# Edge sort of a four-layer graph network: where the spare copies, the norm rows and the factors run, and which bits lie next to each other

## The chip, the cores and the metric

One Trainium2 chip, one core. The metric is the device time of one execution of the whole kernel in microseconds. The kernel runs four graph layers in one launch.

## The reference

100000 nodes have 64 features each; 50000 edges come with a source, a target (sorted by target) and 16 attributes. Four layers follow each other, every one with a residual and a normalization over the 64 features:

```python
edge_index = jnp.stack([src, dst])
x = _layernorm(x + _L0_gnn_ref(x, L0_gnn_W, L0_gnn_c, edge_index), axis=-1)
x = _layernorm(x + _L1_gnn_ref(x, src, dst, L1_gnn_W1_1, L1_gnn_W2_1, L1_gnn_W1_2, L1_gnn_W2_2), axis=-1)
x = _layernorm(x + _L2_gnn_ref(x, edge_index, L2_gnn_W, L2_gnn_att_src, L2_gnn_att_dst, L2_gnn_bias), axis=-1)
x = _layernorm(x + _L3_gnn_ref(x, edge_index, edge_attr_16, batch0, L3_gnn_W, L3_gnn_a), axis=-1)
```

The first layer is an attention in hyperbolic space (it needs, for every node, a chain of norms, tanh and artanh), the second a convolution, the third and fourth attentions with a softmax over the edges that share a target. All of them need sums over the edges of one source or of one target. That is why the kernel sorts the edges once at its start: the stages behind it walk edges in sorted order.

## The kernel before, in words

The change lies in one stage, `order_edges`, from 73 to some 1385 us of the trace. Ahead of it the inputs' constants are set up; behind it come the edge stages of the four layers, whose code is the same in both kernels. The next stage begins with POOL's gathers from the table `T` by edge (lines 1892 and 1895).

**Two sorts.** The edges are sorted by source (order 1, first) and by target (order 0). 65536 slots lie as 128 partitions x 512 columns; each slot has a key and two payload words (the other end, and a contribution of the attributes), in `sort_key` and `sort_load`. A bitonic network of 16 levels has 136 steps; both sorts make 272 steps. `class Network` (line 344) lists the steps as (level, bit) and gives the distance of partners within a row; `COLUMN_BIT` (line 341) says which column bit stands for which bit of the slot number. A bit that is a partition bit is brought into the columns by a **turn**: TensorE transposes 12 blocks of 128 x 128 (line 923 for the key) and ScalarE lands them back in SBUF (`land`, lines 986 to 994). There are 28 turns.

**One step on VectorE** (`order_keys` line 640, `order_loads` line 656): `swap` = low > high (line 652), the two new halves of the key by min and max (653, 654), then two predicated copies of the payload: low <- high where swapped (665), high <- `sort_spare` where swapped (667). `sort_spare` is a copy of the low half made beforehand, by ScalarE (`spare_copy`, line 1001; in a turn's step the landing writes it too, line 992). At the start of each level `flip` (lines 631, 634, 638) computes a sign and multiplies the key by it.

**Work beside the sort.** The first layer needs statistics of every node: 98 chunks of 1024 nodes pass through TensorE (`turned_rows`, `projected`, `added`, `nodes`) and ScalarE (`x_rows` line 1007, squares, `sums_out`, `nodes_out`). A table of steps sets the order by hand: chunk m begins at step `pass_step(m)` = 2m + m//8, and each engine walks the 272 steps and puts the pieces of the chunks behind the step's own work. Every 7 chunks form a batch (`batch_scales` line 737, `batch_roots`), then their **norm rows** (the normalized x of 1024 nodes) are made: 2 chunks of 3 by ScalarE (line 1043, eight activations each), one by VectorE (line 744, `by_vector`). When all batches are done, VectorE computes the **factors** of all nodes (line 754): a chain of 102 VectorE instructions over 128 x 784, some of which hand a function to ScalarE and wait for it. That is step 215 (`FACTORED`).

**Filing.** SP issues the transfers by the same table of steps: chunk loads (`pr_x`), x rows into the table `T` and one id column per chunk (`file_x`, lines 540 and 541, 4-byte words from `sort_node_f`), norm rows in and out (`pl_x`, `X`), factor columns. After a sort `rank` (line 669) puts keys and payload in plain order, `file_keys` (line 487) stores them by three DMAs and reads neighbours back, and `lay_out` (line 677) makes indices from them. For the first sort that is step 145 (`LAID`). It yields `home_row`; POOL then writes 393 times 128 words into `T` (`file_homes`, line 164), which needs all x rows and id columns filed. The stage ends when VectorE has laid out the second sort, POOL's home writes have landed and SP's transfers are done.

## Time and profile before

| | |
|---|---|
| three runs, us | 8039.57, 8034.38, 8027.68 |
| median of the runs, us | 8034.38 |
| the profiled execution: span, us | 8027.0 |
| busy over the span: VectorE / POOL / TensorE / ScalarE | 69% / 66% / 37% / 36% |
| mean DMA rate | 108 GB/s |

All rows below come from the profiled execution of the one core. Engines: PE is TensorE, PEld its weight load, DVE VectorE, ACT ScalarE, POOL GpSimd, SP the queue that issues most transfers. L665 is line 665 of the kernel. A row of the timeline has the start in us from the span's begin, the duration, engine, line, operation, output <- inputs, shape, and in brackets the idle time ahead of it with what ended it. The sort stage is the first sixth of the span, so shares over the whole span say little of it; the rows are taken from its own stretches.

### The profile page before, as it was taken

Reading aid. Unit: us, or ns where it says so; the run is one execution under the profiler, and the core shown is the slowest. Engines: PE = TensorE matmul, PEld = TensorE weight load, DVE = VectorE, ACT = ScalarE, POOL = GpSimd, SP = SyncE. Lnnn points to the kernel's source line nnn. Section 1 sums busy time; section 2 is a strip of 40 time slices with the busy share of each in tenths; the row PEclk is TensorE's granted clock in tenths of the full one; section 3 lists DMA queues with packets and bytes.
Section 4 is the critical chain, followed back from the end, with each engine's and each line's share of the span. In section 5 each row is a group of like instructions: output and inputs, shape, how many; then the busy total and the mean of one; then the engine's idle time right before and its main releaser. Section 6 shows DMA issues by size and latency. Waiting matters only on the chain. (4 is left out here: it accounts for less than half of the span.)

```text
span 8027.0 us, 77025 instructions
## 1 busy us (share of the span) xinstructions
PE 2987.5 (37%) x14049; PEld 2387.9 (30%) x14049; DVE 5509.6 (69%) x16229; ACT 2914.7 (36%) x6536; POOL 5303.4 (66%) x5145
## 2 busy tenths in 40 slices
PE   4776700211111115766656635454400000263322
PEld 1222200211111115666646634454400000252221
DVE  6667687877767756777779969999734444473764
ACT  3555523433333334444435536666500000121211
POOL 0003773777777767777757737777567777777677
PEclk9888855555555557778856655555555555576555
DMA  9884218111111114555569944444321111663321
GB/s 101 110 117 98 68 18 63 27 26 26 26 25 25 25 39 141 168 163 167 160 212 327 328 159 148 146 151 151 126 62 44 45 45 45 132 226 114 97 91 61
DMA packets 786581, 864.04 MB, mean 108 GB/s; under 512 B 469875, under 2 KB 483427, under 8 KB 779804
## 3 DMA queue, kind: packets, MB, share of 16 engines
q1 hardware_dynamic: 572556, 684.47, 30.9%
q0 software_dynamic: 163408, 175.42, 10.5%
q10 hardware_dynamic: 50240, 0.60, 0.6%
q14 instruction: 321, 2.63, 0.1%
q8 instruction: 56, 0.92, 0.1%
HBM read 419.15 MB, written 480.23 MB: 112 GB/s over the span
## 5 line engine op out<-in xcount | busy, mean ns | idle before, releaser
L164 POOL DMA_INDIRECT T<-slot_at,home_row x393 | 434.4, 1105 | 818.4 <-DVE home_row L728 677.9
L1244 POOL DMA_INDIRECT e_other<-X,index x392 | 428.1, 1092 | 177.3 <-issue 117.4
L1232 POOL DMA_INDIRECT e_ahead<-XA,index x392 | 416.3, 1062 | 178.6 <-issue 118.8
L1892 POOL DMA_INDIRECT e_mine<-T,index x392 | 392.3, 1001 | 206.1 <-issue 114.3
L3012 POOL DMA_INDIRECT e_got<-G,index x392 | 411.6, 1050 | 176.7 <-issue 112.9
L3634 POOL DMA_INDIRECT out_rows<-e4s_out,index x392 | 416.8, 1063 | 165.2 <-issue 118.8
L2383 PE MATMUL e_turned<-ident,e_own_x 128*128 128x128 f32 x196 | 54.6, 434 | 1229.4 <-DVE e_own_x L1971 1229.4
L1904 POOL DMA_INDIRECT X<-e_row,index x392 | 419.0, 1069 | 125.3 <-issue 118.8
L2532 POOL DMA_INDIRECT e_got<-X,index x392 | 413.6, 1055 | 119.5 <-issue 119.5
L2529 POOL DMA_INDIRECT e_mine<-X,index x392 | 404.4, 1032 | 130.4 <-issue 119.2
L3443 POOL DMA_INDIRECT rows<-X,index x392 | 395.6, 1009 | 130.6 <-issue 130.6
L1255 POOL DMA_INDIRECT XA<-e4d_sent,index x392 | 391.0, 998 | 119.4 <-issue 118.8
L1244 POOL DMA_INDIRECT e4d_other<-X,index x392 | 376.1, 959 | 136.1 <-issue 118.2
L1895 POOL DMA_INDIRECT e_other<-T,index x392 | 385.2, 983 | 119.5 <-issue 119.5
L2383 PEld LDWEIGHTS e_turned<-ident,e_own_x 128*128 128x128 f32 x196 | 35.1, 217 | 1240.0 <-DVE e_own_x L1971 970.6
L665 DVE COPY_PREDICATED sort_load<-sort_swap,sort_load 128x512 f32<-128x512 int32 x272 | 229.8, 845 | 250.3 <-ACT sort_spare L1001 213.7
L1703 ACT ACTIVATE e_z<-e_mine,e_share 128x64 f32<-128x64 f32 x1572 | 380.7, 334 | 35.2 <-DVE e_share L1563 35.0
L1776 PE MATMUL e_back<-w_heads,e_z_t 128*128 128x66 f32 x1600 | 329.8, 401 | 121.2 <-ACT e_z_t L1712 121.2
L1783 PE MATMUL e4d_spread<-e4d_diag,ones 128*128 128x128 f32 x2 | 0.8, 502 | 976.7 <-DVE e4d_diag L1603 976.7
L1776 PEld LDWEIGHTS e_back<-w_heads,e_z_t 128*128 128x128 f32 x1600 | 321.1, 311 | 137.9 <-ACT e_z_t L1712 106.2
L1765 PE MATMUL e_z_turned<-ident,e_z 128*128 128x128 f32 x800 | 181.1, 420 | 457.0 <-DVE e_z L1586 457.0
L1521 DVE SCALAR_TENSOR_TENSOR e_state<-e_state,e_ex,e_pay 128x64 f32<-128x64 f32 x1568 | 320.9, 279 | 0.0
(685 smaller groups left out, 13023.6 us busy)
## 6 DMA issues: line engine op xcount, KB each, us to landing
XA<-e_n_xa SPq DMA_DIRECT2D x49, 1056.0 KB, 5.5
SUMS<-e_state SPq DMA_DIRECT2D x49, 1056.0 KB
e4n_n_xa<-XA SPq DMA_DIRECT2D x49, 1056.0 KB, 5.3
X<-e_n_row SPq DMA_DIRECT2D x49, 576.0 KB
X<-pl_x SPq DMA_DIRECT2D x98, 268.0 KB, 3.0
e_n_x<-X SPq DMA_DIRECT2D x49, 536.0 KB
B<-e_n_b SPq DMA_DIRECT2D x49, 528.0 KB
e_n_b<-B SPq DMA_DIRECT2D x49, 528.0 KB
```

The lines of the kernel that those rows point to most:

```text
L164: gp.indirect_dma_start(out=words, out_offset=bass.IndirectOffsetOnAxis(ap=home_row[:, t:t + 1], axis=0), in_=slot_at[:, t:t + 1], in_offs ...
L1232: gp.indirect_dma_start(out=ahead[:, b, j, :], out_offset=None, in_=g.XA[0:SLOTS, :], in_offset=bass.IndirectOffsetOnAxis(ap=index_of(g, 0 ...
L1244: gp.indirect_dma_start(out=other[:, h, j, :], out_offset=None, in_=others[:, :], in_offset=bass.IndirectOffsetOnAxis(ap=index_of(g, s, 1, ...
L1255: gp.indirect_dma_start(out=target[:, :], out_offset=bass.IndirectOffsetOnAxis(ap=index_of(g, s, 2, n, j), axis=0), in_=sent[:, h, j, :], ...
L1776: last = t.matmul(back[:, j // 4, (j % 4) * (D + 2):(j % 4 + 1) * (D + 2)], lhsT=z_t[:, 2 * j + q, :], rhs=g.w_heads[:, q, :], start=(q == ...
L1892: gp.indirect_dma_start(out=mine[:, h, j, :], out_offset=None, in_=g.T0[:, :], in_offset=bass.IndirectOffsetOnAxis(ap=index_of(g, s, 0, n, ...
L1904: gp.indirect_dma_start(out=g.X1[:, :], out_offset=bass.IndirectOffsetOnAxis(ap=index_of(g, s, 2, n, j), axis=0), in_=row[:, h, j, :], in_ ...
L2529: gp.indirect_dma_start(out=mine[:, h, j, :], out_offset=None, in_=g.X1[:, :], in_offset=bass.IndirectOffsetOnAxis(ap=index_of(g, s, 0, n, ...
L2532: gp.indirect_dma_start(out=got[:, h, j, :], out_offset=None, in_=g.X1[:, :], in_offset=bass.IndirectOffsetOnAxis(ap=index_of(g, s, 1, n, ...
L3012: gp.indirect_dma_start(out=got[:, h, j, :], out_offset=None, in_=g.G2[:, :], in_offset=bass.IndirectOffsetOnAxis(ap=index_of(g, s, 1, n, ...
L3443: gp.indirect_dma_start(out=g.rows[:, n * J + j, :], out_offset=None, in_=g.X3[:, :], in_offset=bass.IndirectOffsetOnAxis(ap=index_of(g, s ...
L3634: gp.indirect_dma_start(out=out_rows[:, :], out_offset=bass.IndirectOffsetOnAxis(ap=index_of(g, s, 2, n, j), axis=0), in_=out[:, h, j, :], ...
```

## The change

Parts, all within `order_edges` and `Network`:

1. **Spare copies on VectorE.** The copy of the low half is now a VectorE instruction behind `swap` (new line 690); in a turn's step it follows the key's max, once the last word has landed. ScalarE's `land` has three activations instead of five.
2. **Which bits lie close.** A level's steps now use the partition order up to level 9 and the turned order above it only for the bits that then need it; the two shortest distances, 1 and 2, occur in 12 of the 272 steps (60 before). The turns stay 28. Blocks of a turn are now taken (`block`) or landed (`laid`) with a stride of four columns, in one of the two directions.
3. **Norm rows** are all on ScalarE; VectorE's two instructions per chunk (lines 744 on) are gone, and the order of ScalarE's side work around turns is changed.
4. **Passes are spread**: `pass_step(m)` = 2m + 2m//5 instead of 2m + m//8.
5. **Factors in two halves**, at steps 124 and 241, of 128 x 392 each, instead of one at step 215. Factor columns follow each half.
6. **Filing.** `file_keys` is issued from ScalarE's queue, with four part DMAs for each of the three tables. SP issues one id column per step (`blank_homes`) and the x rows on every other step; POOL's home writes wait for the id columns alone.

```diff
+    @staticmethod
+    def by_column(level, m):
+        return level > IN_COLS and m >= BY_COLUMN
...
     def distance(self, n):
-        m = self.steps[n][1]
-        return 1 << (m - IN_COLS if m >= IN_COLS else COLUMN_BIT[m])
+        level, m = self.steps[n]
+        if not self.by_column(level, m):
+            return BLOCKS << m if m < BY_COLUMN else 1 << (m - BY_COLUMN)
+        if m < IN_COLS:
+            return P << (m - BY_COLUMN)
+        return BLOCKS << (m - IN_COLS) if m < LEVELS - 2 else 1 << (m - LEVELS + 2)
...
     def pass_step(m):
-        return 2 * m + m // 8
+        return 2 * m + 2 * m // 5
...
-    FACTORED = batch_step(CH // BATCH - 1) + 2
+    HALF = CH // 2
+    FACTORED = [batch_step(HALF // BATCH - 1) + 2, batch_step(CH // BATCH - 1) + 2]
...
-                engine.dma_start(table.rearrange("(p t) a -> p (t a)", p=EC), ordered[0:EC, w, :]).then_inc(written[s], 16)
-            engine.wait_ge(written[s], 16 * 5)
+                for h in range(FILED):
+                    rows = table[h * LANES * COLS:min((h + 1) * LANES * COLS, EP), :].rearrange("(p t) a -> p (t a)", t=COLS)
+                    engine.dma_start(rows, ordered[h:h + BLOCKS * (rows.shape[0] - 1) + 1:BLOCKS, w, :]).then_inc(written[s], 16)
+            engine.wait_ge(written[s], 16 * (2 + 3 * FILED))
...
                 for n in range(-8, STEPS):
                     for m in passed(n + 8):
                         x_in(m)
-                        for c in range(3 * m // 2, min(3 * (m + 1) // 2, CH)):
-                            file_x(c)
+                    if 0 <= n < CH:
+                        blank_homes(n)
+                    if 0 <= n < 2 * CH and n % 2:
+                        file_x(n // 2)
...
-                gp.wait_ge(filed_x, 16 * (2 * CH + 1))
+                gp.wait_ge(home_blank, 16 * CH)
                 gp.wait_ge(home_rows, 1)
...
                     compared.done(v.tensor_tensor(net.kept(swap[:, :].unsqueeze(1), n)[:, 0], low[:, 0], high[:, 0], ALU.is_gt), "swap")
+                    if n not in turns:
+                        spare_copy(n)
                     compared.done(v.tensor_tensor(new_low[:, 0], low[:, 0], high[:, 0], ALU.min), "low_key")
                     compared.done(v.tensor_tensor(new_high[:, 0], low[:, 0], high[:, 0], ALU.max), "key")
+                    if n in turns:
+                        v.wait_ge(landed.sem, landed.after(turns[n], "contrib"))
+                        spare_copy(n)
+
+                def spare_copy(n):
+                    copied.done(v.tensor_copy(net.kept(spare[:, :, :], n), net.halves(load[net.order(n)][:, :, :], n)[0]))
...
-                        copy = a.activation(net.kept(spare[:, w:w + 1, :], n), net.halves(turned[:, 1 + w:2 + w, :], n)[0], ACT.Copy)
-                        landed.done(a.activation(load[s][:, w, :], turned[:, 1 + w, :], ACT.Copy), name)
-                    copied.done(copy)
+                        landed.done(a.activation(net.laid(load[s][:, w, :], n), net.landing(turned[:, 1 + w, :]), ACT.Copy), name)
...
+                    if n in turns:
+                        land(n)
+                        side_work(n - 1)
+                    if n + 1 not in turns:
+                        side_work(n)
+                    if n == LENGTH + 2:
+                        file_keys(a, 1)
+                file_keys(a, 0)
```

How instructions move, at three places. The first is VectorE in steps 46 and 47 (level 10, bits 8 and 7), before: two steps of five instructions each. `sort_swap` is the mask, `sort_spare` the copy of the low half, `sort_load` the payload.

```order
L652 TENSOR_TENSOR sort_swap<-sort_key 128x256
L653 TENSOR_TENSOR sort_key<-sort_key 128x128x2
L654 TENSOR_TENSOR sort_key<-sort_key 128x128x2
L665 COPY_PREDICATED sort_load<-sort_swap,sort_load 128x256x2
L667 COPY_PREDICATED sort_load<-sort_swap,sort_spare 128x256x2
L652 TENSOR_TENSOR sort_swap<-sort_key 128x256
L653 TENSOR_TENSOR sort_key<-sort_key 128x256
L654 TENSOR_TENSOR sort_key<-sort_key 128x256
L665 COPY_PREDICATED sort_load<-sort_swap,sort_load 128x512
L667 COPY_PREDICATED sort_load<-sort_swap,sort_spare 128x512
```

The same steps on VectorE now:

```order
L680 TENSOR_TENSOR sort_swap<-sort_key 128x256
L690 COPY sort_spare<-sort_load 128x512
L683 TENSOR_TENSOR sort_key<-sort_key 128x256
L684 TENSOR_TENSOR sort_key<-sort_key 128x256
L699 COPY_PREDICATED sort_load<-sort_swap,sort_load 128x2x256
L701 COPY_PREDICATED sort_load<-sort_swap,sort_spare 128x2x256
L680 TENSOR_TENSOR sort_swap<-sort_key 128x256
L690 COPY sort_spare<-sort_load 128x512
L683 TENSOR_TENSOR sort_key<-sort_key 128x2x128
L684 TENSOR_TENSOR sort_key<-sort_key 128x2x128
L699 COPY_PREDICATED sort_load<-sort_swap,sort_load 128x4x128
L701 COPY_PREDICATED sort_load<-sort_swap,sort_spare 128x4x128
```

The copy has come into VectorE's own queue, and the runs of neighbouring elements (2 in the first step before) are 256 and 128 long.

The second place is ScalarE around the first turn, before. `sort_turned` are the transposed blocks, `pr_xt` a chunk's rows on their way to TensorE, `pl_x` norm rows.

```order
L1007 ACTIVATE pr_xt<-pr_turned,eps 128x512
L989 ACTIVATE sort_key<-sort_turned 128x512
L992 ACTIVATE sort_spare<-sort_turned 128x256
L993 ACTIVATE sort_load<-sort_turned 128x512
L992 ACTIVATE sort_spare<-sort_turned 128x256
L993 ACTIVATE sort_load<-sort_turned 128x512
L1043 ACTIVATE pl_x<-pl_x,pl_offset,pl_inverse 128x64 x8
```

And now:

```order
L1024 ACTIVATE pr_xt<-pr_turned,eps 128x512
L1060 ACTIVATE pl_x<-pl_x,pl_offset,pl_inverse 128x64 x8
L1015 ACTIVATE sort_key<-sort_turned 128x512
L1018 ACTIVATE sort_load<-sort_turned 128x512 x2
L1046 ACTIVATE node_stats<-pr_by_node 128x40
L1042 ACTIVATE pr_sums<-pr_summed 10x512
```

A turn's landing is three activations, and the side work of the step before the turn follows it.

The third place is SP in the middle of the first sort, before. `pr_x` is a chunk's load, `T<-in_x` x rows, `T<-sort_node_f` an id column, `pl_x` and `X` the norm rows in and out.

```order
L501 DMA pl_x<-in_x 128x512
L501 DMA pr_x<-in_x 128x512
L540 DMA T<-in_x 1024x64
L541 DMA T<-sort_node_f 1024x1x1
L501 DMA pl_x<-in_x 128x512
L516 DMA X<-pl_x 128x536
L501 DMA pr_x<-in_x 128x512
L540 DMA T<-in_x 1024x64
L541 DMA T<-sort_node_f 1024x1x1
L540 DMA T<-in_x 1024x64
L541 DMA T<-sort_node_f 1024x1x1
```

And now:

```order
L522 DMA pl_x<-in_x 128x512
L560 DMA T<-sort_node_f 1024x1x1 x2
L564 DMA T<-in_x 1024x64
L522 DMA pl_x<-in_x 128x512
L537 DMA X<-pl_x 128x536
L522 DMA pr_x<-in_x 128x512
L560 DMA T<-sort_node_f 1024x1x1 x2
L564 DMA T<-in_x 1024x64
L537 DMA X<-pl_x 128x536
L522 DMA pr_x<-in_x 128x512
```

Id columns now come two for one row copy.

## Rows read from the trace of the kernel before

**Rows 1.** Windows of two stretches of the sort: busy time by engine, clock, DMA.
```profile
core 0: us, PE busy (x) PEld busy (x) DVE busy (x) ACT busy (x) POOL busy (x), PEclk, DMA share, GB/s
73.00:723.00 650.00, 463.31 (x1384) 172.89 (x1385) 459.63 (x874) 352.78 (x831) 0.09 (x1) 0.86 0.87 111
...
1019.00:1166.00 147.00, 1.86 (x8) 1.46 (x8) 131.16 (x110) 19.55 (x22) 114.18 (x99) 0.50 0.02 2
```
**Rows 2.** Groups of VectorE, 73 to 1364 us: busy, mean ns, idle ahead.
```profile
L665 DVE COPY_PREDICATED sort_load<-sort_swap,sort_load 128x512 f32<-128x512 int32 x272 | 229.8, 845 | 250.3 <-ACT sort_spare L1001 213.7 <-ACT sort_load L993 35.5
...
L771 DVE TENSOR_SCALAR sort_work<-sort_work 128x784 f32<-128x784 f32 x25 | 14.5, 581 | 4.4 <-ACT sort_work L1051 3.7
...
L634 DVE TENSOR_SCALAR sort_sign<-sort_bit 128x512 f32<-128x512 int32 x31 | 13.4, 433 | 1.1
```
**Rows 3.** Timeline at 98 us: start, us, engine, line, idle before.
```profile
98.68 0.61 ACT L1001 ACTIVATE sort_spare<-sort_load 128x512 f32<-128x512 f32 x1
...
99.39 0.71 DVE L665 COPY_PREDICATED sort_load<-sort_swap,sort_load 128x512 f32<-128x512 int32 x1 [2.45 <-ACT sort_spare L1001]
```
**Rows 4.** Timeline of VectorE in an undisturbed step, 1356 us.
```profile
1356.50 0.43 DVE L652 TENSOR_TENSOR sort_swap<-sort_key 128x256 int32<-128x256 f32 x1
1356.84 0.42 DVE L653 TENSOR_TENSOR sort_key<-sort_key 128x256 f32<-128x256 f32 x1
...
1359.05 0.43 DVE L652 TENSOR_TENSOR sort_swap<-sort_key 128x256 int32<-128x256 f32 x1
```
**Rows 5.** Line 164, POOL's home writes: shortest/median/longest ns, first and last start.
```profile
L164 POOL DMA_INDIRECT T<-slot_at,home_row x393: 966/1021/1947, 722.9 to 1296.8; - x197
```
**Rows 6.** Tile sort_load, its second predicated copy and its ranking copy.
```profile
L667 DVE COPY_PREDICATED sort_load<-sort_swap,sort_spare x272: 696/727/1311, 76.4 to 1363.4; 128x512 f32<-128x512 int32 x136
...
L674 DVE COPY sort_work<-sort_load x4: 598/603/606, 678.4 to 1365.2; 128x512 f32<-128x512 f32 x4
```
**Rows 7.** Timeline of POOL where the next stage begins.
```profile
1384.80 0.99 POOL L1892 DMA_INDIRECT e_mine<-T,index  x1 [87.00 <-DVE e_state L1928]
1386.09 0.95 POOL L1895 DMA_INDIRECT e_other<-T,index  x1 [0.30 <-issue]
```
**Rows 8.** Timeline of VectorE at a level's start, 1306 us: flip, then the predicated copy.
```profile
1306.41 0.42 DVE L631 TENSOR_SCALAR sort_bit<-sort_gray 128x512 int32<-128x512 int32 x1
...
1307.93 0.73 DVE L665 COPY_PREDICATED sort_load<-sort_swap,sort_load 128x512 f32<-128x512 int32 x1
```
**Rows 9.** Timeline at a turn, 1336 us.
```profile
1336.57 1.97 PE L923 MATMUL sort_turned<-ident,sort_load 128*128 128x128 f32 x8 [1.43 <-DVE sort_load L667]
...
1339.54 1.30 DVE L665 COPY_PREDICATED sort_load<-sort_swap,sort_load 128x512 f32<-128x512 int32 x1 [1.82 <-ACT sort_load L993]
```
**Rows 10.** Timeline of VectorE: the factors' first instruction, and the next step's swap.
```profile
1023.97 1.54 DVE L776 TENSOR_TENSOR sort_work<-node_stats 128x784 f32<-128x784 f32 x1
...
1165.99 0.43 DVE L652 TENSOR_TENSOR sort_swap<-sort_key 128x256 int32<-128x256 f32 x1 [0.22 <-DVE node_cols L771]
```
**Rows 11.** Timeline of VectorE where the first sort is laid out.
```profile
716.32 0.28 DVE L688 TENSOR_SCALAR lay_diag<-ident,sort_work 128x128 f32<-128x128 f32 x1
```
**Rows 12.** DMA issues, 73 to 723 us: engine, op, count, KB each, us to landing.
```profile
T<-in_x SPq DMA_DIRECT2D x92, 256.0 KB, 8.5
pr_x<-in_x SPq DMA_DIRECT2D x69, 256.0 KB
X<-pl_x SPq DMA_DIRECT2D x50, 268.0 KB, 3.7
pl_x<-in_x SPq DMA_DIRECT2D x52, 256.0 KB, 6.5
T<-sort_node_f SPq DMA_DIRECT2D x93, 4.0 KB, 8.9
```
**Rows 13.** Groups of ScalarE, 73 to 1364 us: the norm rows.
```profile
L1043 ACT ACTIVATE pl_x<-pl_x,pl_offset,pl_inverse 128x64 f32<-128x64 f32 x528 | 181.3, 426 | 5.0 <-DMA pl_x<-in_x 5.0
```
**Rows 14.** Groups of POOL beside the factors, 1019 to 1166 us.
```profile
L164 POOL DMA_INDIRECT T<-slot_at,home_row x99 | 114.2, 1153 | 32.8 <-issue 32.8
```
**Rows 15.** Line 1007, ScalarE's row copies of the 98 passes: first and last start.
```profile
L1007 ACT ACTIVATE pr_xt<-pr_turned,eps x98: 662/662/693, 72.8 to 995.2; 128x512 f32<-128x512 f32 x98
```

More of the change, by code:

```diff
@@ L338, in set_up @@
     sem.clear()
-COLUMN_BIT = (7, 8, 2, 3, 4, 5, 6, 0, 1)
+BY_COLUMN = 7
+BLOCKS = COLS // P
+LANES = P // BLOCKS
+FILED = -(-EC // LANES)
 class Network:
@@ L375, in kept, with block, laid, landing @@
         return tile.rearrange("p w (g d) -> p w g d", d=self.distance(n))
+    def block(self, tile, n, b):
+        if self.by_column(*self.steps[n]):
+            return tile.rearrange("p (c b) -> p b c", b=BLOCKS)[:, b, :]
+        return tile[:, b * P:(b + 1) * P]
+    def laid(self, tile, n):
+        if self.by_column(*self.steps[n]):
+            return tile.rearrange("p (b c) -> p b c", b=BLOCKS)
+        return tile.rearrange("p (c b) -> p b c", b=BLOCKS)
+    def landing(self, blocks):
+        return blocks.rearrange("p (b c) -> p b c", b=BLOCKS)
 def order_edges(nc, g, src, dst, l3_a, attr, x, sem):
@@ L398, in normed @@
         return [m for m in range(CH) if 23 + 5 * m // 2 == n]
-    FACTORED = batch_step(CH // BATCH - 1) + 2
-    assert FACTORED + CH // 2 < STEPS and all(23 + 5 * m // 2 >= batch_step(m // BATCH) + 2 for m in range(CH))
+    HALF = CH // 2
+    FACTORED = [batch_step(HALF // BATCH - 1) + 2, batch_step(CH // BATCH - 1) + 2]
+    assert FACTORED[1] + HALF // 2 < STEPS and all(23 + 5 * m // 2 >= batch_step(m // BATCH) + 2 for m in range(CH))
     def passed(n):
@@ L658, in order_loads @@
                     v.wait_ge(compared.sem, compared.after(n, "swap"))
-                    if n in turns:
-                        v.wait_ge(landed.sem, landed.after(turns[n], "contrib"))
                     v.wait_ge(copied.sem, copied.after(n))
@@ L884, in _ @@
                 for n in range(STEPS):
-                    if n == FACTORED:
-                        v.wait_ge(scaled.sem, scaled.after(CH // BATCH - 1, "offset"))
-                        factors()
+                    if n in FACTORED:
+                        half = FACTORED.index(n)
+                        v.wait_ge(scaled.sem, scaled.after((half + 1) * HALF // BATCH - 1, "offset"))
+                        halves_asked.append(len(asked))
+                        factors(half)
                     order_keys(n)
@@ L915, in turn @@
                     for b in range(COLS // P):
-                        last = t.transpose(turned[:, 0, b * P:(b + 1) * P], key[s][:, (n - 1) % 2, b * P:(b + 1) * P], g.ident[:, :])
+                        last = t.transpose(turned[:, 0, b * P:(b + 1) * P], net.block(key[s][:, (n - 1) % 2, :], n, b), g.ident[:, :])
                     turned_pe.done(last, "key")
@@ L988, in land @@
                     a.wait_ge(turned_pe.sem, turned_pe.after(k, "key"))
-                    landed.done(a.activation(key[s][:, (n - 1) % 2, :], turned[:, 0, :], ACT.Copy), "key")
+                    landed.done(a.activation(net.laid(key[s][:, (n - 1) % 2, :], n), net.landing(turned[:, 0, :]), ACT.Copy), "key")
                     for w, name in enumerate(("other", "contrib")):
                         a.wait_ge(turned_pe.sem, turned_pe.after(k, name))
-                        copy = a.activation(net.kept(spare[:, w:w + 1, :], n), net.halves(turned[:, 1 + w:2 + w, :], n)[0], ACT.Copy)
-                        landed.done(a.activation(load[s][:, w, :], turned[:, 1 + w, :], ACT.Copy), name)
-                    copied.done(copy)
-                def spare_copy(n):
-                    if n:
-                        a.wait_ge(compared.sem, compared.after(n - 1, "high"))
-                    else:
-                        a.wait_ge(made, 5)
-                    copied.done(a.activation(net.kept(spare[:, :, :], n), net.halves(load[net.order(n)][:, :, :], n)[0], ACT.Copy))
+                        landed.done(a.activation(net.laid(load[s][:, w, :], n), net.landing(turned[:, 1 + w, :]), ACT.Copy), name)
                 def x_rows(m):
@@ L1044, in norm_rows, with side_work @@
                     x1_act.done(last)
-                a.wait_ge(x1_ones, 3)
-                for n in range(STEPS):
-                    if n == FACTORED:
-                        for i, (out, x_in, f, f_scale, f_bias) in enumerate(asked):
-                            a.wait_ge(to_act, i + 1)
-                            a.activation(out, x_in, f, bias=f_bias, scale=f_scale).then_inc(from_act, 1)
-                    if n in turns:
-                        land(n)
-                    else:
-                        spare_copy(n)
+                def side_work(n):
                     for m in passed(n - 6):
@@ L1067, in _ @@
                     for m in normed(n):
-                        if not by_vector(m):
-                            norm_rows(m)
+                        norm_rows(m)
+                a.wait_ge(x1_ones, 3)
+                for n in range(STEPS):
+                    if n in FACTORED:
+                        half = FACTORED.index(n)
+                        for i in range(halves_asked[half], (halves_asked + [len(asked)])[half + 1]):
+                            out, x_in, f, f_scale, f_bias = asked[i]
+                            a.wait_ge(to_act, i + 1)
+                            a.activation(out, x_in, f, bias=f_bias, scale=f_scale).then_inc(from_act, 1)
+                    if n in turns:
[6 more added lines that the diff above has]
+                file_keys(a, 0)
     sem.clear()
```

87 lines of the change are left out of this document (37 added, 50 removed).

## The prediction

> **What bounds the kernel now.** I read the stretches of the sort stage first [rows 1]. From 73 to 723 us VectorE works 459.6 of 650 us, ScalarE 352.8 and TensorE 463.3: no engine is full, so something waits. The groups say for what: the first predicated copy of a step (L665) has 250.3 us of VectorE's idle time ahead of it, 213.7 of them until ScalarE's spare copy [rows 2]. One such wait [rows 3]: the spare copy stands in ScalarE's queue behind a pass's row copies, starts at 98.68, and VectorE resumes at 99.39 after 2.45 us. So VectorE's 272 steps are tied to ScalarE's pass work. An undisturbed step takes 2.55 us from swap to swap [rows 4] and 2.57 over the distances from 4 up.
>
> A second chain runs beside it. POOL's 393 home writes (L164) begin when step 145 has laid out the first sort, at 722.9, and the last starts at 1296.8 [rows 5]; the sort goes on to 1363.4 [rows 6], and the next stage's first gather starts at 1384.80 [rows 7]. POOL sits idle 87 us before that. So the stage now ends with VectorE, and POOL is 87 us behind it. The question is when each chain ends after the change.
>
> **VectorE up to step 145.** From the first swap at 73:
> - 146 steps x 2.57 = 375 us.
> - Spare copies: each frees VectorE after its duration less 0.08, as the swap's 0.43 does after 0.34 [rows 4]. Before shows no VectorE spare copy. The nearest rows are a one-input pass over 512 elements, 0.433 (L634) [rows 2], and a copy of 512 that gathers with a stride, 0.603 (L674) [rows 6]. Nearly all new distances have runs of 4 or more, so I take 0.43: 146 x 0.35 = 51; at 0.60 it is 25 more. The 213.7 us of waiting goes with them.
> - Rare bits: a predicated copy is 1.31 at distances 1 and 2 against 0.73 [rows 6], 1.17 us for a step's two. Steps at these distances fall from 60 to 12. Six lie here: 7. The 48 that go save 56 us over both sorts.
> - 20 sign flips, 1.52 each (from 1306.41 to the predicated copy at 1307.93) [rows 8]: 30, as before.
> - 14 turns: the predicated copy waits 1.82 us for the landed words [rows 9], and the key's landing adds some 0.4. ScalarE now lands three tiles instead of five, but VectorE's copy follows the last: I keep 2.2 each, 31.
> - 8 batch scales at about 1: 8.
> - Half of the factors. The whole is 142.0 us (1023.97 to 1165.99) [rows 10]: 102 VectorE instructions in a chain. 0.433 us for 512 and 0.581 for 784 [rows 2] give 0.15 fixed, 0.19 with the gap. So half costs (142 - 19)/2 + 19 = 81, and 85 with ScalarE's round trips, whose fixed part is not halved. The two halves cost 28 more than the whole did; the first now lies ahead of POOL's start.
> - Ranking and layout: 8 (the layout alone from 716.32 to 722.9) [rows 5, 11].
>
> Sum 595, so 668 without a wait. What can be late now is TensorE at a turn, for want of x rows. Before, 356 transfers of the five kinds listed took 0.87 of 650 us of the DMA engines [rows 1, 12], 1.6 us each. In steps 0 to 97 the new SP order issues 98 id columns, 49 row copies, 45 pass loads and some 60 norm transfers: 252 x 1.6 = 400 us, against 98 steps at 3.4 = 333 us and a prefetch of 8 steps, 27 us. That is up to 40 us of stall; zero if the 4 KB id columns cost less than the mean. I take 20, and 10 for turns that meet TensorE amid a pass: **home rows at about 700** (668 to 740).
>
> **ScalarE.** 33 more norm rows x 8 activations x 0.343 (the 0.426 each [rows 13], overlapped) add 91 us, and the 244 spare copies and 56 half ones leave it. VectorE sheds 64 products and sums of norm rows in exchange. Both lie off the path except through the pass loop (below). Keys filed from ScalarE's queue cost 9 more issues per sort, about 3.5 us; the first sort's are covered by seven steps (some 20 us) ahead of the layout, the last by POOL. If POOL were earlier, 3.5 us would show.
>
> **POOL.** 393 writes. Beside the factors, where VectorE is 89% busy, 99 took 1.153 + 0.33 = 1.485 us each [rows 1, 14]; gathers of the next stage stand 1.29 apart [rows 7]. VectorE will be nearly full, so I take 1.485: 584, and 6 for landing: **end at 1290**. The next gather follows in about 6 us (the last landing, the barrier, a few clears): 1296.
>
> **VectorE's own end.** From 700, 126 steps x 2.92 = 368, shorts 7, 11 flips 17, 14 turns 31, batches 6, the other half 85, waits 10: 1224. The tail behind the last step is 21 us before (1363.4 + 0.7 to 1384.8) and 3.5 more now: 1248. POOL ends last.
>
> So the stage closes 1384.8 - 1296 = 89 us sooner; later stages compute the same tables and I leave them. The profiled span is 8027.0, 7.4 us under the median of 8034.4; against the median: 8034.4 - 89 = **7945 us**.
>
> **Rivals.**
> - *VectorE still ends the stage* (0.12). If writes come at 1.36 us or less, POOL is done by 1248. For: POOL's pace without VectorE beside it is 1.29. Against: with VectorE at 89% it was 1.485. Time 8034.4 - 137 = 7898.
> - *The spare copies hold POOL back* (0.12). About one copy of 0.43 falls on every two writes. If each held a write by half its length or so, a write takes 1.60: 700 + 629 + 12 = 1341, time 7990. For: the writes are longest beside the factors, which have many one-input operations (1.153 against a shortest of 0.966) [rows 5, 14]. Against: 39 of those in 142 us moved the mean by only a little. The Trainium skill (SBUF — State Buffer, Who interferes with whom) says that a VectorE copy in its two-port mode takes the port pair that POOL needs to write DMA descriptors, and that the later one blocks fully. By that rule each meeting costs the rest of the copy, about this rival's time; the trace shows the direction, not the size.
> - *The pass loop is slowed, and this is slower* (0.07). The first half of the factors needs 49 passes. With p us per pass, home rows are at 73 + 49p + 12 (last batch) + 85 + 22 steps at about 3.6 (80) + 7 = 257 + 49p, and the stage ends 596 later. That passes 1384.8 from p = 10.9. At 12 the time is 8090. Before, p was (995.2 - 72.8)/97 = 9.5 [rows 15]. For: all norm rows now stand in ScalarE's queue, and DMA may starve the loop. Against: ScalarE no longer waits for VectorE at each step.
> - *It does not do what it says* (0.04): copies at 0.60 and waits of 80 us put home rows at 775, the end at 1371 and the time within 16 us of before.
>
> **Numbers.** The forecast case has 0.65. Its own range is 7885 (home rows 675, writes at 1.41) to 8000; the lock rival and VectorE's end lie inside, so 7885 to 8008 leaves out the slower rival and the edge of the last. 0.2% is 16 us, about what a measurement of this kernel tells from no change: faster by more 0.88, within 0.05, slower 0.07.
>
> **What would show it.** Right: no idle time of L665's successor until ScalarE except at 28 turns; a COPY of about 0.43 x272 on VectorE; first home write near 700; writes near 1.49 apart, the last near 1285; VectorE done 40 us or more before the next gather, then idle until POOL. Wrong: home writes start after 760 (the pass loop or DMA), writes at 1.6 (the port), or VectorE still busy when POOL is done.

## The result, and the profile after

The changed kernel takes 7921.16 us (median of four runs, 7918.86 to 7926.57) against 8033.76 before: a ratio of 0.9864, interval [0.985, 0.9878]. The forecast was 7945 in a range of 7885 to 8008. The profiled execution has a span of 7919.9 us, 107.1 less than before. Both chains of the sort stage moved: the home rows are there at 679.3 instead of 722.9, the second sort is ranked at 1196.8 instead of 1364.2, and the next stage's first gather starts at 1267.16 instead of 1384.80 [rows 7], 117.6 sooner. The later stages, whose code is the same, gave back 10.5 of it, a little here and there.

Windows of the changed kernel: busy time by engine, TensorE's clock, DMA share, GB/s, as in [rows 1].

```profile
73.00:420.00 347.00, 256.56 (x857) 98.10 (x856) 308.37 (x657) 204.52 (x497) 0.00 (x0) 0.93 0.85 117
73.00:679.00 606.00, 381.92 (x1242) 145.02 (x1242) 529.03 (x1085) 321.81 (x775) 0.00 (x0) 0.85 0.69 103
```

VectorE now works 529 of 606 us up to the home rows, where it worked 459.6 of 650. The groups of VectorE from 73 to 1364 us show what became of the wait [rows 2]:

```profile
L699 DVE COPY_PREDICATED sort_load<-sort_swap,sort_load 128x512 f32<-128x512 int32 x272 | 201.3, 740 | 2.9
L690 DVE COPY sort_spare<-sort_load 128x512 f32<-128x512 f32 x272 | 125.9, 463 | 25.3 <-ACT sort_load L1018 25.2
```

The 250.3 us of idle time ahead of the first predicated copy are 2.9. What is left, 25.2, stands ahead of the copy in the 28 turns. The copies cost 125.9 us in all. One undisturbed step, in the timeline:

```profile
126.85 0.42 DVE L680 TENSOR_TENSOR sort_swap<-sort_key 128x256 int32<-128x256 f32 x1
127.19 0.42 DVE L690 COPY sort_spare<-sort_load 128x512 f32<-128x512 f32 x1
...
129.80 0.43 DVE L680 TENSOR_TENSOR sort_swap<-sort_key 128x256 int32<-128x256 f32 x1
```

It is 2.95 us from swap to swap, against 2.55 [rows 4]. POOL's home writes and the gather behind them, by line and in the timeline [rows 5, 7] (where a distance between writes is given below, it is the last start less the first, over 392):

```profile
L164 POOL DMA_INDIRECT T<-slot_at,home_row x393: 967/1091/1721, 679.3 to 1257.7; - x197
```

```profile
1267.16 0.99 POOL L1916 DMA_INDIRECT e_mine<-T,index  x1 [8.52 <-DVE e_state L1952]
```

Before, POOL stood idle for 87 us here; now for 8.52. VectorE had laid out the second sort at 1218 and waited 47 us. **POOL ends the stage**, as forecast.

One thing was not forecast. ScalarE's queue around the filing of the first sort's keys, and what VectorE did meanwhile:

```profile
639.20 2.57 ACTq L513 DMA_DIRECT2D contribs<-sort_work  x4
647.60 1.53 ACTq L516 DMA_DIRECT2D sort_work<-keys  x3
...
651.94 0.69 ACT L1024 ACTIVATE pr_xt<-pr_turned,eps 128x512 f32<-128x512 f32 x1 [15.05 <-issue]
...
654.65 0.50 DVE L774 RECIPROCAL pl_inverse<-pl_inverse 128x56 f32<-128x56 f32 x1 [12.88 <-ACT pl_inverse L1052]
```

Between the stores (L513) and the read-backs (L516) ScalarE waits until the stores have landed. It does no other work for 15.05 us. Behind that wait stand the roots of the batch of step 139, and VectorE needs them: it waits 12.88 us at 654.65, on the path to the home rows.

### The profile page after: what moved, and what is told of

Same layout as the page of the kernel before. It is cut to its first block and busy times, and to the rows that moved or that the text cites. A ratio compares the mean times of both kernels' runs of the same rounds, so it can differ in the third digit from the quotient of the medians.

```text
span 7919.9 us, 77310 instructions
## 1 busy us (share of the span) xinstructions
PE 2935.9 (37%) x14049; PEld 2367.6 (30%) x14049; DVE 5526.6 (70%) x16542; ACT 2879.4 (36%) x6509; POOL 5343.8 (67%) x5146
## 5 line engine op out<-in xcount | busy, mean ns | idle before, releaser
L1789 PEld LDWEIGHTS e_z_turned<-ident,e_z 128*128 128x128 f32 x800 | 162.7, 225 | 461.1 <-DVE e_z L1610 384.0
```

## The experiments

The time before varied from 8032.9 to 8039.9 us between the chips of the groups, so times are compared by their ratio to the kernel before on the same chip. "After" is the changed kernel, from which every experiment starts; they are called e1 to e12 in the order in which they stand.

### The spare copies back on ScalarE

```diff
-                    if n not in turns:
+                    if n not in turns and not (n < STEPS):
                         spare_copy(n)
...
+                def spare_copy(n):
...
+                    copied.done(a.activation(net.kept(spare[:, :, :], n), net.halves(load[net.order(n)][:, :, :], n)[0], ACT.Copy))
...
+                    elif n < STEPS:
+                        spare_copy(n)
```

> Only the place of the spare copies is put back: in the 244 steps without a turn ScalarE makes them, as before the change; everything else is as changed. Theory (VectorE was tied to ScalarE's pass work): a step falls from 2.92 to 2.57 us, but the waits come back. Before they were 213.7 us over 272 steps, 0.79 each, so 132 plain steps of the first sort lose 0.44 each, 58 us: home rows at about 735 instead of 679.3, time about 7975 (7950 to 8010). Rival (the gain came from the bits and the halved factors, and the spread passes leave ScalarE time enough): no waits, 132 x 0.35 = 46 us gained, home rows at about 633, time about 7875.

Measured: 7959.0 us, ratio 0.9902 [0.9886, 0.9919], some 30 us slower than after. The group of VectorE (73 to 1300 us) and POOL's two rows:

```profile
L699 DVE COPY_PREDICATED sort_load<-sort_swap,sort_load 128x512 f32<-128x512 int32 x272 | 202.8, 746 | 186.0 <-ACT sort_spare L1025 182.5
```

```profile
L164 POOL DMA_INDIRECT T<-slot_at,home_row x393: 969/977/1650, 723.5 to 1276.5; - x197
```

```profile
1299.26 0.99 POOL L1925 DMA_INDIRECT e_mine<-T,index  x1 [21.80 <-DVE e_state L1961]
```

The waits come back, 182.5 us of the 213.7 before, and the home rows are 44 us later (58 expected). The rival, that spread passes leave ScalarE time enough, falls. But the writes stand 1.4106 us apart instead of 1.4755, and the stage is now ended by VectorE: POOL is idle for 21.8 us. That gave a suspicion on the copies, which two further runs took up.

### The order of the bits back

`Network`, the slot numbers, `rank` and the key filing as before; `block`, `laid` and `landing` without a stride.

> Only the order of the bits is put back: 60 steps at distances 1 and 2 instead of 12, plain blocks in the turns, key filing in three DMAs. Theory (price of a short distance 1.17 us a step): 24 more such steps in the first sort, 28 us, and 24 spare copies that gather with a stride, 0.18 more each, 4: home rows at about 711, last write and stage end 32 later, time about 7953 (7945 to 7960). Rival (the strided landing and block reads of the turns cost as much as the short distances save): home rows within 8 us of 679.3, time 7915 to 7930.

Measured: 7938.4 us, ratio 0.9873 [0.9857, 0.989].

```profile
L164 POOL DMA_INDIRECT T<-slot_at,home_row x393: 969/1092/1717, 690.2 to 1271.6; - x197
```

The home rows are 10.9 us later, a third of the 32 of the theory, and more than the rival's 8. The price of a short step was right: a predicated copy takes 1.29 to 1.30 at distances 1 and 2, and the 24 more such steps cost 28 us. But other waits shrank: outside the factors VectorE's plain steps of the first sort lost 25 us (ranking and layout included) instead of 42. The plain landings are also cheaper. Two rows of ScalarE's groups, 73 to 679 us, of this kernel and of after:

```profile
L997 ACT ACTIVATE sort_load<-sort_turned 128x512 f32<-128x512 f32 x28 | 16.2, 596 | 18.8 <-PE sort_turned L928 18.8
```

```profile
L1018 ACT ACTIVATE sort_load<-sort_turned 128x512 f32<-128x512 f32 x28 | 22.2, 855 | 7.7 <-PE sort_turned L949 7.6
```

On average the landing of a tile costs 0.26 us more. Only every other turn writes with a step of four columns: in after such a landing of the payload takes 1.11 us, a plain one 0.60. The new bit order is worth about 11 us here, not 28.

### The keys read back two steps later

```diff
                     if n == LENGTH + 2:
                         file_keys(a, 1)
+                    if n == LENGTH + 4:
+                        read_keys(a, 1)
```

`read_keys` is the wait for the written keys and the five read-backs, cut out of `file_keys`.

> Only ScalarE's wait for the written keys of the first sort and the five read-backs behind it move, from step 138 to step 140, behind that step's batch roots; the writes stay at 138. Theory (VectorE's 12.88 us in front of the batch's reciprocal come from ScalarE standing 15 us in that wait): the wait of VectorE goes to under 2 us, home rows at about 666.5, time about 7908. Rival (the batch waits for the passes anyway, or the layout then waits for the read-back): home rows within 4 us of 679.3, time 7917 to 7925.

Measured: 7916.2 us, ratio 0.9844 [0.9827, 0.986].

```profile
646.84 0.50 DVE L776 RECIPROCAL pl_inverse<-pl_inverse 128x56 f32<-128x56 f32 x1 [2.37 <-ACT pl_inverse L1054]
```

```profile
L164 POOL DMA_INDIRECT T<-slot_at,home_row x393: 967/1095/1718, 671.5 to 1249.5; - x197
```

The wait falls from 12.88 to 2.37 us and ranking to home rows from 58.2 to 47.7. The first sort itself was ranked 2.7 us later in this execution, so the home rows came 7.8 sooner and the next gather (1258.99) 8.2. That ScalarE's wait caused VectorE's is shown.

### The first half of the factors behind the layout

```diff
-    FACTORED = [batch_step(HALF // BATCH - 1) + 2, batch_step(CH // BATCH - 1) + 2]
+    FACTORED = [LAID + 1, batch_step(CH // BATCH - 1) + 2]
```

> Only the first half of the factors moves, from step 124 to step 146, behind the layout of the first sort. Theory (POOL ends the stage and starts when the home rows are there): home rows 83 us sooner, at about 596; POOL's last write at about 1175, then VectorE ends the stage: its layout of the second sort stays at about 1218, next gather at about 1221 instead of 1267.2, time about 7875 (7865 to 7885). Rival (SP stands in front of the factor columns with the chunk loads behind it, so the passes come late and the second half of the factors with them): VectorE's end moves out by 20 to 80 us, time 7895 to 7955.

Measured: 7897.7 us, ratio 0.9826 [0.981, 0.9842].

```profile
L164 POOL DMA_INDIRECT T<-slot_at,home_row x393: 970/1117/1708, 589.8 to 1172.1; - x197
```

```profile
1240.48 0.99 POOL L1916 DMA_INDIRECT e_mine<-T,index  x1 [67.32 <-DVE e_state L1952]
```

POOL is done at 1172, as forecast (1175), and then waits 67 us: VectorE ends the stage, and later than the theory said (1240.5, not 1221). Two new waits account for it, 12.03 us here and 12.51 at 816.6, and a group of TensorE (670 to 790 us) names their cause:

```profile
780.17 0.50 DVE L774 RECIPROCAL pl_inverse<-pl_inverse 128x56 f32<-128x56 f32 x1 [12.03 <-ACT pl_inverse L1052]
```

```profile
L957 PE MATMUL pr_turned<-ident,pr_x 128*128 128x128 f32 x44 | 9.0, 339 | 33.8 <-DMA pr_x<-in_x 31.5 <-ACT pr_xt L1024 2.1
```

TensorE waits 31.5 us for chunk loads. They stand in SP's queue among the 49 factor columns. Theory and rival each had half.

### The changed kernel again

> The changed kernel itself, beside the others of this group, for the spread between chips and runs: home rows within 3 us of 679.3, next gather within 4 us of 1267.2, ratio to the kernel before 0.985 to 0.988.

Measured: 7926.2 us, ratio 0.986 [0.9844, 0.9877], home rows at 679.2, next gather at 1267.5. The next gather agrees with after's to 0.4 us. The profiled execution is 14.9 us longer, 14.6 of them behind that gather, in the later stages.

### Each copy twice beside POOL

```diff
+                    if n > LAID:
...
+                        copied2.done(v.tensor_copy(net.kept(work[:, 0:2, 0:COLS // 2], n), net.halves(load[net.order(n)][:, :, :], n)[0]))
                     copied.done(v.tensor_copy(net.kept(spare[:, :, :], n), net.halves(load[net.order(n)][:, :, :], n)[0]))
```

> From step 146 on each spare copy of VectorE is made twice (the first into unused memory): 126 more copies beside POOL's writes, none before them. VectorE's end moves 126 x 0.35 = 44 us: second ranking at about 1241 instead of 1196.8. Theory (a VectorE copy holds POOL's write by about 0.2 us: without the copies the writes stood 1.4106 apart, with them 1.4755, 25 us over the stretch): writes 1.54 apart, last at about 1283, time about 7946 (7938 to 7955). Rival (there the writes were quicker because VectorE stood waiting for ScalarE, not because the copies were gone): writes within 0.015 of 1.4755, last within 6 us of 1257.7, and VectorE's own end of about 1266 sets the stage, time 7918 to 7928.

Measured: 7917.7 us, ratio 0.9848 [0.9832, 0.9864].

```profile
L164 POOL DMA_INDIRECT T<-slot_at,home_row x393: 969/1037/1636, 679.7 to 1229.6; - x197
```

```profile
1261.56 0.99 POOL L1921 DMA_INDIRECT e_mine<-T,index  x1 [30.51 <-DVE e_state L1957]
```

The theory missed, and so did the rival's pace. With twice the copies POOL is *quicker*: 1.4028 us a write, the last at 1229.6, 28 us sooner. VectorE's end moved out as worked out (ranked at 1236.9), and ends the stage, as the rival had it. So more copies need not slow POOL; what one costs depends on when a write meets it (last section).

### The copy as a minimum

```diff
-                    copied.done(v.tensor_copy(net.kept(spare[:, :, :], n), net.halves(load[net.order(n)][:, :, :], n)[0]))
+                    low = net.halves(load[net.order(n)][:, :, :], n)[0]
+                    if n > LAID:
+                        copied.done(v.tensor_tensor(net.kept(spare[:, :, :], n), low, low, ALU.min))
...
```

This holds from step 146 on.

> From step 146 on the spare copy of VectorE is the minimum of the low half with itself, an operation with two inputs, in place of a copy. By the flip's product of 512 it takes 0.69 instead of 0.42, so VectorE's end moves 126 x 0.27 = 34 us: second layout at about 1252. Theory (it is the form with one input that holds POOL): writes 1.41 apart, last at about 1232, and VectorE ends the stage, next gather at about 1256, time about 7909 (7902 to 7916). Rival (any operation of VectorE holds POOL by a share of its length): writes 1.49 to 1.51 apart, last at 1263 to 1271, next gather 1273 to 1281, time 7925 to 7937.

Measured: 7931.0 us, ratio 0.9866 [0.985, 0.9883].

```profile
L164 POOL DMA_INDIRECT T<-slot_at,home_row x393: 969/1167/1510, 680.4 to 1267.0; - x197
```

1.4963 us a write, next gather at 1276.5: inside the rival's numbers. With one copy, two copies or none (after, e6, e1) the pace was 1.476, 1.403 and 1.411, so neither the number nor the length of VectorE's operations gives the pace by itself. That any operation can hold a write, as the rival says, is borne out in the last section; that it costs a share of its length is not.

### The late half with its columns paced

The edits of e3 and e4 together, and the first half's columns later in SP's order.

```diff
-                        for m in range(2 * (n - factored_at), 2 * (n - factored_at) + 2):
+                        filed_at = 184 if h == 0 else factored_at
+                        for m in range(2 * (n - filed_at), 2 * (n - filed_at) + 2):
```

> Three edits together: the read-back of the first sort's keys behind the batch roots of step 140, the first half of the factors at step 146, and its 49 columns issued by SP from step 184 on instead of right behind it. Theory (what the half behind the layout lost, 12.6 us at step 173 and 12.6 at step 180, was the chunk loads that stood behind the columns): these two waits go to under 3 us each, VectorE's layout of the second sort is done at about 1205, POOL's last write at about 1165, next gather at about 1208, time about 7862 (7852 to 7875). Rival (the pass loop is late by the half itself, in which ScalarE stands, whatever SP issues): 20 to 25 us of waits stay, next gather 1228 to 1234, time 7882 to 7890.

Measured: 7876.3 us, ratio 0.98 [0.9783, 0.9816]. Steps 173 and 180 take 4.44 and 4.82 us where they took 16.70 and 17.04 in e4, so the columns in front of the chunk loads were the cause (the edit of e3 lies 33 steps ahead of them). But the columns now issued from step 184 on made another chunk load late:

```profile
889.87 0.43 DVE L683 TENSOR_TENSOR sort_swap<-sort_key 128x256 int32<-128x256 f32 x1 [9.62 <-ACT sort_key L1018]
```

With this the next gather starts at 1222.96, not at 1208.

### Norm rows in thirds

Every third chunk of norm rows back on VectorE, with the two operations of before.

> Only the norm rows are put back as before: every third chunk on VectorE, two operations of 0.69 each, two of three on ScalarE. Theory (VectorE's own work sets both chains): 16 such chunks lie ahead of the home rows, 1.4 each, 22 us; ScalarE's relief gives back up to 8 of it at turns and batches: home rows at 693 to 702, next gather later by as much, time about 7941 (7934 to 7949). Rival (the 91 us of norm rows weigh on ScalarE, which the turns wait for): the waits at turns and batches fall by more than 16 us, home rows at 685 or sooner, time 7927 or less.

Measured: 7917.3 us, ratio 0.9856 [0.9839, 0.9872]: no difference from after that can be told.

```profile
L164 POOL DMA_INDIRECT T<-slot_at,home_row x393: 966/1067/1647, 686.6 to 1259.5; - x197
```

The home rows are 7.3 us later, 22 being the price of the added work; VectorE's idle time ahead of them fell by 11.2 (77.1 to 65.9). The writes stand 1.4613 apart, so POOL's last is only 1.8 later. The theory missed, and the rival narrowly (it asked for home rows at 685 or sooner and more than 16 us of waits gone). For the time it does not matter here which engine makes the norm rows, but only because POOL ends the stage: VectorE ranks the second sort at 1224.9, 28 us later than in after.

### The x rows sooner

```diff
-                    if 0 <= n < 2 * CH and n % 2:
-                        file_x(n // 2)
+                    if 0 <= n < CH:
+                        file_x(n)
```

> Only SP's order changes: the 98 copies of x rows go out in steps 0 to 97, one a step, instead of in steps 1 to 195. That is 49 more transfers of 256 KB in the first 98 steps. Theory of the prediction (1.6 us each, prefetch 27 us): 78 us more load, where 85% of 347 us are taken already, so chunk loads come late and VectorE waits for them at turns and batches: home rows 20 to 50 us later, at 700 to 730, time 7940 to 7970. Rival (the pass loop has slack, or TensorE and ScalarE set it): home rows within 8 us of 679.3, time 7915 to 7930.

Measured: 7994.0 us, ratio 0.9948 [0.9932, 0.9965]: some six tenths of the gain are gone.

```profile
73.00:420.00 347.00, 238.38 (x728) 87.49 (x726) 265.28 (x565) 166.89 (x407) 0.00 (x0) 0.85 1.16 120
```

```profile
L164 POOL DMA_INDIRECT T<-slot_at,home_row x393: 966/1102/1722, 750.3 to 1330.3; - x197
```

The DMA share of the first 347 us goes from 0.85 to 1.16 and the home rows come 71 us later. The added load was put at 78 us; nearly as much shows, more than the 20 to 50 expected. VectorE's new waits stand ahead of turns: at the ends of steps 54, 65, 83 and 104 it waits 12.1 to 14.6 us each. The path was not the one of the theory. TensorE waited only 12.9 us for chunk loads from 73 us to the home rows; it is ScalarE that stands, 125.6 us in 27 waits, each in front of a chunk's norm rows. One of them, ahead of the turn at step 55:

```profile
273.86 2.76 ACT L1060 ACTIVATE pl_x<-pl_x,pl_offset,pl_inverse 128x64 f32<-128x64 f32 x8 [9.35 <-issue]
...
276.53 0.57 ACT L1015 ACTIVATE sort_key<-sort_turned 128x512 f32<-128x512 f32 x1
...
277.13 0.43 DVE L680 TENSOR_TENSOR sort_swap<-sort_key 128x256 int32<-128x256 f32 x1 [12.14 <-ACT sort_key L1015]
```

SP had issued the load for this chunk's norm rows 8.7 us before, at 265.2; in the other waits too ScalarE starts 6 to 10 us behind the issue. That it waits for the load is read from these distances, and one of the waits (5.25 us) the trace puts down to it by name. In after the load of the same chunk was issued 17.8 us ahead, and ScalarE did not wait. Behind the norm rows in ScalarE's queue stands the turn's landing, and behind that VectorE.

### The passes at the old rate

```diff
-        return 2 * m + 2 * m // 5
+        return 2 * m + m // 8
```

> Only the table of passes is put back, 2m + m//8: the first half of the factors then stands at step 111 and the second at step 215, and chunk loads come 2.125 steps apart instead of 2.4. Theory (the passes, at 9.5 us each before, cannot follow steps of 2.93 us at that rate): VectorE waits at turns and batches of the first sort 15 to 40 us more, home rows at 694 to 720, time 7936 to 7961. Rival (spreading did nothing): home rows within 6 us of 679.3, time 7917 to 7930.

Measured: 7970.3 us, ratio 0.9922 [0.9905, 0.9938]. A group of VectorE up to 740 us, and the same of after up to 679:

```profile
L680 DVE TENSOR_TENSOR sort_swap<-sort_key 128x256 int32<-128x256 f32 x146 | 62.0, 425 | 68.6 <-ACT sort_key L1015 55.0 <-DVE sort_load L701 0.9 <-DVE node_cols L798 0.2
```

```profile
L680 DVE TENSOR_TENSOR sort_swap<-sort_key 128x256 int32<-128x256 f32 x146 | 62.0, 425 | 28.6 <-ACT sort_key L1015 14.9 <-DVE sort_load L701 0.5 <-DVE node_cols L798 0.2
```

The waits for a turn's key rise from 14.9 to 55.0 us; home rows at 732.4, 53 later (15 to 40 expected). ScalarE's waits for TensorE's node statistics, up to the home rows, rise from 53.6 to 188.8 us: TensorE does not follow, as the theory has it. By the ratios, spreading the passes is worth some four tenths of the whole gain.

### The late half, one column a step

As e8, with one column a step from step 172 on.

> The three edits of the late half again, with its 49 columns issued one a step from step 172 to 220 instead of two a step from 184. Theory (what was left, 9.5 us in front of the turn at step 207, was a chunk load behind the columns): that wait goes to under 4 us, next gather at about 1217 instead of 1223.0, time about 7870 (7864 to 7877). Rival (another stall takes its place): next gather 1221 to 1227, time 7874 to 7881.

Measured: **7862.2 us, ratio 0.9787 [0.9771, 0.9803]**, the quickest version, and a little quicker than the theory. The turn of step 207, which waited 9.62 us, now waits 2.25:

```profile
879.76 0.42 DVE L683 TENSOR_TENSOR sort_swap<-sort_key 128x256 int32<-128x256 f32 x1 [2.25 <-ACT sort_key L1018]
```

```profile
L164 POOL DMA_INDIRECT T<-slot_at,home_row x393: 969/1110/1718, 585.5 to 1177.1; - x197
```

```profile
1210.86 0.99 POOL L1922 DMA_INDIRECT e_mine<-T,index  x1 [32.81 <-DVE e_state L1958]
```

POOL now waits 33 us for VectorE; the two chains have changed places, and the stage ends 56 us sooner than in after.

## Why the prediction was right, and where its terms were off

**The mechanism held.** VectorE's steps came loose from ScalarE's queue, POOL's writes became the end of the stage, and they began when VectorE had the home rows. e1 shows the first, the 8.52 us that POOL now waits where [rows 7] had 87.00 the second, e4 the third (home rows 89.5 us sooner, last write 85.6 sooner).

**The home rows were put at 700 and came at 679.3.** By the steps of the changed trace, in us:

| term | forecast | measured |
|---|---|---|
| 146 steps of 2.57 with the copy's 0.35 | 426 | 426 |
| short distances | 7 | 7 |
| sign flips | 30 | 30 |
| 14 turns, and their meeting a pass | 31 + 10 | 32 |
| 8 batch scales | 8 | 20 |
| half of the factors | 85 | 83 |
| ranking and layout | 8 | 8 |
| stalls for want of chunk loads | 20 | none |

The step that failed is "*up to 40 us of stall; zero if the 4 KB id columns cost less than the mean. I take 20*". They do cost less. In after TensorE waited for no chunk load from 73 us to the home rows; the first such wait is 3.8 us at 714.7. Up to step 98 (409 us) the forecast had 400 us of DMA work; the window to 420 us has 0.85 of 347, that is 295. The packets of 4 bytes, nearly all of them id columns of 1024, took 76.8 us of the 16 engines up to 679 us, about 0.8 us a column: half of the 1.6 that was charged. For the large transfers 1.6 fits e10, where 78 us of added load delayed the home rows by 71, though through the norm rows and not the chunk loads. The second failure hides in a sum that came out well: "*the first sort's are covered by seven steps (some 20 us) ahead of the layout*". I looked at who needs the keys and not at what stands behind the wait in ScalarE's queue. The batch roots did; e3 takes back 10.5 of these 12 us. A small slip had no effect: 32 chunks of norm rows moved to ScalarE, not 33, which is 88 us of work and not 91.

**POOL's pace was put at 1.485 and was 1.4755**, for a reason that does not hold. It was taken from the stretch beside the factors, because VectorE would be nearly full there too. e6 filled VectorE further and POOL became quicker. The number was near by luck. In all, the next gather came 28.8 us before the 1296 of the forecast, 20.7 of them by the home rows and 8.1 by POOL's stretch.

**The rivals.** That VectorE would end the stage (0.12) missed by 47 us of its idle time; its end, forecast at 1248, came at 1218 for the layout and some 3 us of clears. The rival in which copies hold POOL (0.12) had a real hold and the wrong count: a copy does hold a write that begins inside it, but in after only 11 of the 393 writes began inside one, and lost 1.1 us in all. The pass loop (0.07) did not slow: the passes were 9.5 us apart in [rows 15] and are (980.0 - 58.5)/97 = 9.5 now. But e11 shows that the danger was real: at the old rate VectorE's waits grew from 15 to 55 us at the turns' keys and from 16 to 25 at the batches.

**After the sort.** The forecast left the later stages alone; they took 10.5 us more in the profiled execution and 5 by the medians. That is within what they vary: two executions of the changed kernel, after and e5, differ there by 14.6.

**The parts do not add up.** Undone one at a time they cost, by the ratios: the copies 0.0038 (31 us), the bits 0.0009 (7, too little for the times to tell; its next gather is 14.0 later), the spread passes 0.0058 (47), the norm rows nothing. Doubling the rate of x rows alone costs 0.0084 (67). The gain of 0.0136 needs VectorE loose from ScalarE, and passes and transfers thin enough that the quicker steps are not caught by them; the halving of the factors was not tried apart.

## What to carry to other kernels

When an engine's private copy frees a chain of small steps, look next at what the steps will overtake: here the rate at which passes and transfers are issued decided more than the copy itself. A wait for a DMA inside a queue costs what stands behind it, not what it is for; issue the stores, do other work, then wait. When two chains end a stage, move work from ahead of the handover to behind it (e4, e12), and expect the queue it brings along, factor columns in this case, to become the next wait.

## What the runs showed of the hardware

**A write's length depends on when it starts.** POOL and VectorE in the changed kernel, from one stretch of the timeline:

```profile
894.20 0.42 DVE L690 COPY sort_spare<-sort_load 128x512 f32<-128x512 f32 x1
894.31 1.15 POOL L164 DMA_INDIRECT T<-slot_at,home_row  x1 [0.30 <-issue]
...
897.05 1.02 POOL L164 DMA_INDIRECT T<-slot_at,home_row  x1 [0.30 <-issue]
...
898.15 0.72 DVE L699 COPY_PREDICATED sort_load<-sort_swap,sort_load 128x512 f32<-128x512 int32 x1
898.38 1.31 POOL L164 DMA_INDIRECT T<-slot_at,home_row  x1 [0.31 <-issue]
...
899.99 1.03 POOL L164 DMA_INDIRECT T<-slot_at,home_row  x1 [0.30 <-issue]
...
901.09 0.72 DVE L699 COPY_PREDICATED sort_load<-sort_swap,sort_load 128x512 f32<-128x512 int32 x1
901.32 1.31 POOL L164 DMA_INDIRECT T<-slot_at,home_row  x1 [0.30 <-issue]
```

From 897 us on two writes fit one step of 2.94 us, and the second of each step begins 0.23 us behind the start of a predicated copy and takes 1.31. Counted over all 393 writes of each kernel (number, mean us):

```
                 within 0.3 us behind a         all others
                 predicated copy's start
before            46   1.39                     347   1.07
after            104   1.37                     289   1.05
e1, no copies     57   1.30                     336   1.03
e6, two copies    16   1.34                     377   1.05
e7, minimum       89   1.38                     304   1.08
```

But the predicated copy is not the only one that holds a write. A write that begins while VectorE is idle takes 0.97 us (71 writes in after). The one at 894.31 begins 0.11 us into a *spare copy*, with 0.3 of it left, and takes 1.15. All fourteen traces together, for writes that began at least 0.06 us into an instruction of the sort step or a reciprocal of the factors and batches, with more than 0.2 us of it left (number, mean us that were left, mean us the write took above 0.97):

```
spare copy                              106   0.28   0.16
compare, minimum, maximum of the key    816   0.28   0.16
predicated copy of 0.7 us              1224   0.50   0.35
reciprocal                              300   1.17   0.00
```

So a write waits for what is left of the instruction, less 0.125 us (0.156 for a predicated copy); in the first three groups over 99% lie within 0.03 us of that. Of these, the reciprocal alone does not hold it. Added up over the 393 writes, the time above 0.97 is 53.2 us before, 64.6 in after, 39.1 in e1, 36.8 in e6 and 70.9 in e7. e6's is 27.8 shorter than after's, and its last write came 28.1 sooner.

What differs is how often a write meets an instruction early. Of the steps under 4.5 us between the first and the last write, 92 of 110 hold two writes in after, 84 of 103 in e7, but 43 of 98 in e6, where 48 hold three. A step of 2.94 us seems to lock two writes into a bad phase; with two copies the step is about 3.3 us and the writes drift past; with the minimum two fit again, and more of the loss lies beside the key's three instructions (21.2 us, 11.1 in after). So doubling the copies could make POOL quicker, and the pace could not be read from how full VectorE is. The shorter holds are measured; that the step's length makes the lock is argued from these counts, and no run varied it alone.

The rule of the prediction (the Trainium skill, SBUF — State Buffer, Who interferes with whom), that a VectorE copy locks POOL out, agrees with these traces: a write that meets a copy waits for the rest of it, less 0.125 us. Another rule of the same section, that a VectorE instruction with two SBUF inputs contends with a POOL instruction that reads SBUF, agrees too: the key's instructions and the predicated copies hold the write, the reciprocal with its one input does not.

**The copy pays as well.** The spare copy took 420 ns on average up to the home rows and 512 beside POOL's writes. Two rows of VectorE's groups, 73 to 679 and 679 to 1197 us:

```profile
L690 DVE COPY sort_spare<-sort_load 128x512 f32<-128x512 f32 x146 | 61.4, 420 | 13.9 <-ACT sort_load L1018 13.8
```

```profile
L690 DVE COPY sort_spare<-sort_load 128x512 f32<-128x512 f32 x126 | 64.6, 512 | 11.4 <-ACT sort_load L1018 11.4
```

The 64 of these 126 that began 0.5 us or more into a write took 0.60 us on average, most of them ending 0.25 us behind the write's end; the other 62 took 0.42. The step's other five instructions kept their mean to 6 ns.

**Every 113th write waits.** In all fourteen traces POOL stood 3 to 10 us behind the 113th, 226th and 339th write (3.01, 2.97 and 7.30 us in after), whatever VectorE did.
